# A retention kernel: the low halves of the masked scores are summed on GpSimd before the row-sum matmul

## The chip, the cores and the metric

The kernel runs on one core of one Trainium2 chip, as one program. The metric is the device time of one execution in microseconds. Engines are named PE or TensorE (matrix products), PEld (its weight loads), DVE or VectorE, ACT or ScalarE, POOL or GpSimd, and SP or SyncE (it only issues DMAs here).

## The reference

The input is 8 sequences of 512 tokens with 256 features in float32. Four layers of retention with a feed-forward part run over it, then one mixture of 8 experts. The part that the change touches is in `_retention`:

```python
k, q, v = jnp.split(x @ wkqv, 3, axis=-1)
qkt = jnp.einsum('bid,bjd->bij', q, k) / jnp.sqrt(jnp.float32(d))
row_norm = 1.0 + jnp.sqrt(jnp.arange(s, dtype=x.dtype))[None, :, None]
r = jnp.tril(qkt) / row_norm
denom = jnp.clip(jnp.abs(r.sum(-1, keepdims=True)), 1.0, None)
r = r / denom
return jnp.einsum('bij,bjd->bid', r, v)
```

Each row of the causal scores is divided by the size of its sum. In a layer, the result goes through a gated projection, a group norm over the whole sequence, a residual sum, a GELU feed-forward part and a layer norm:

```python
a, gate = jnp.split(r @ w1 + b1, 2, axis=-1)
y = _groupnorm1(a * jax.nn.silu(gate) @ w2 + b2, gg, gb) + h
f = jax.nn.gelu(y @ wf1 + bf1_) @ wf2 + bf2_
return _layernorm(f + y, lg, lb)
```

## The kernel before

**Precision.** Every float32 operand of a large product is split in two: a high half (ScalarE copies it to the type fp32r) and a low half (the operand less the high half, by VectorE or GpSimd). `mm3` makes a product of three matmuls: high by high, weights high by low, weights low by high.

**Tiling.** A sequence of 512 tokens is one *slot* of a step; a step handles two, slot A (number 0) and slot B (number 1). Four pairs of sequences and four layers make 16 steps. Slot A of a step is interleaved with the later parts of slot B of the step before, and slot B with the later parts of slot A of the same step. Each engine has its own instruction stream, with the order written out in its `body(now, before, seam)`; engines wait for one another on counting semaphores. `first` is step 0 without a step before it, `seam` marks the first step of layers 1 to 3, where new weights are made, and `tail` finishes what the last step left.

**Scores.** `scores` makes the transposed scores in four blocks of 128 keys (partitions) by queries (free axis). Because of the causal mask, block b needs queries from `LO[b]` on only: `LO = [0, 128, 256, 256]`, so widths 512, 384, 256, 256. ScalarE writes the high half `pf_sp[s][0]` (L470), VectorE the low half `pf_sp[s][1]` (L623), and GpSimd's `mask_scores` (L336) clears the part above the diagonal in both halves, block by block, and counts `p_masked[s]` up by one for each block.

**`retain` on TensorE.** It does `weighted_h(0)`, `weighted_h(1)`, then the row sums of the scores with a matrix of ones (`ones_r`, L947: eight matmuls into bank 0, high and low half of each block, `rowsum_psum` when done), then `weighted_h(2)` and `weighted_h(3)`. The row sums wait for `p_masked` of the third block first, later of the fourth. VectorE's `divisor` (L659, L660) takes the row sums, `low_r` the product, `invert` the reciprocal.

**What stands around it.** On TensorE, `retain(A)` is followed by the up projection of B of the step before (it needs `ry_lo` of B, L623 on VectorE), and `retain(B)` by the down projection of A, which takes one chunk of the hidden layer after another as GpSimd's `split_f(A)` (L320, four times) delivers it. Later TensorE does `out_projection(B)`, which needs `tu_lo` of B from VectorE's `gated_products` (`gated` is L677, `low_u` L623).

**GpSimd's order** in a step: `split_h(A)` (L320), mask 0 of A, `rstd_group(B)` (L343), masks 1 to 3 of A, `split_f(B)`, `layernorm_rstd(A)` (L348, L350), `split_h(B)`, `rstd_group(A)`, masks 0 to 3 of B, `split_f(A)`, `layernorm_rstd(B)`, `layernorm_out(A)`, `layernorm_out(B)` (L209, L212 each). `split_weight` makes the low halves of the weights at the seams and in step 0: there the one of `qk` comes first in the step, ahead of `split_h(A)`.

**VectorE** runs `groupnorm_out(B)` (L730 to L740) with `low_y(B)` behind the low halves of A's scores, then `divisor(A)`.

## Time and profile before

| | |
|---|---|
| runs of the kernel before | 2754.56, 2757.17, 2759.98 us (median 2757.17) |
| the profiled execution, first to last instruction | 2757.3 us |
| retention layers, by the order of time | about 0 to 1180 us |
| TensorE busy, whole span | 95% |
| VectorE, ScalarE, GpSimd busy, whole span | 49%, 49%, 47% |

The page of the profile gives busy times, a picture of the span in 40 slices and the costliest groups. Other views of the same trace are used below: stretches (busy time of each engine in a stretch, with the granted clock of TensorE as a share of full speed), waits (who waited for whom, in total, how often, the longest), groups by shape, and the order of time (start, duration, engine, line, operation, result<-operands, shapes, count, and in brackets the idle time before it and what ended it). Durations of GpSimd operations that follow one another overlap by about 0.04 us. Matmuls are pipelined: the time that one costs is from its start to the start of the next.

### The profile page before, as it was taken

Reading aid. Unit: us, or ns where it says so; the run is one execution under the profiler, and the core shown is the slowest. Engines: PE = TensorE matmul, PEld = TensorE weight load, DVE = VectorE, ACT = ScalarE, POOL = GpSimd, SP = SyncE. Lnnn points to the kernel's source line nnn. Section 1 sums busy time; section 2 is a strip of 40 time slices with the busy share of each in tenths; the row PEclk is TensorE's granted clock in tenths of the full one; section 3 lists DMA queues with packets and bytes.
Section 4 is the critical chain, followed back from the end, with each engine's and each line's share of the span. In section 5 each row is a group of like instructions: output and inputs, shape, how many; then the busy total and the mean of one; then the engine's idle time right before and its main releaser. Section 6 shows DMA issues by size and latency. Waiting matters only on the chain.

```text
span 2757.3 us, 42999 instructions
## 1 busy us (share of the span) xinstructions
PE 2625.7 (95%) x14962; PEld 2292.4 (83%) x14962; DVE 1348.6 (49%) x2432; ACT 1361.9 (49%) x2246; POOL 1301.5 (47%) x1142
## 2 busy tenths in 40 slices
PE   7999999999999999949899999999999999999998
PEld 5788778877888788738798998989989989899997
DVE  2677887777777877757812112121121121211233
ACT  3555555566556555525344444444444444444443
POOL 2244554455445544435345445454454454544454
PEclk8999999999999999966999999999999999999999
DMA  4110020002000100042001001000010000000000
GB/s 153 58 31 30 31 69 31 30 31 69 31 30 31 38 31 23 15 133 70 31 0 33 0 0 33 0 29 5 0 34 0 0 33 0 2 0 0 8 23 31
DMA packets 70774, 82.77 MB, mean 30 GB/s; under 512 B 3104, under 2 KB 65696, under 8 KB 70688
## 3 DMA queue, kind: packets, MB, share of 16 engines
q1 hardware_dynamic: 70560, 81.58, 9.0%
q8 instruction: 55, 0.90, 0.1%
q14 instruction: 31, 0.25, 0.0%
q10 hardware_dynamic: 128, 0.03, 0.0%
HBM read 58.27 MB, written 23.33 MB: 30 GB/s over the span
## 4 chain that ended last, share of the span: by engine, by line
issue 24%; POOL 17%; PE 13%; POOLq 1%; DVE 0%; DMA 0%; ACT 0%; ACTq 0%; DVEq 0%; SPq 0%
POOL hid_lo L1257 17%; PE m_ps L1500 4%; PE m_ps L1501 4%; PE m_ps L1502 4%; DMA xh<-h_store 0%; POOLq L1256 0%; PE m_ps L1519 0%; PE m_ps L1526 0%; DVE x L1358 0%; POOLq L1260 0%; ACT x1T_hi L1302 0%; ACT x1Tf L1301 0%; DVE xh L1370 0%; DVE m_stat L1347 0%; POOL rstd L1236 0%
## 5 line engine op out<-in xcount | busy, mean ns | idle before, releaser
L1257 POOL TENSOR_TENSOR hid_lo<-act,hid_hi 128x512 fp32r<-128x512 f32 x512 | 701.5, 1372 | 759.6 <-ACT act L1329 759.5
L1327 ACT ACTIVATE hid_hi<-m_ps,b_e 128x512 fp32r<-128x512 f32 x512 | 353.4, 690 | 811.4 <-PE m_ps L1502 811.2
L1444 DVE TENSOR_TENSOR tile_out<-m_ps,b_bc 128x512 f32<-128x512 f32 x128 | 82.4, 686 | 1015.9 <-PE m_ps L1502 1015.6
L1329 ACT ACTIVATE act<-m_ps,b_e 128x512 f32<-128x512 f32 x512 | 349.7, 683 | 0.0
L1500 PE MATMUL m_ps<-w_even,hid_hi 128*128 128x256 f32 x1024 | 289.6, 283 | 13.5 <-DVE tile_out L1444 13.0
L1502 PE MATMUL m_ps<-w_even,hid_lo 128*128 128x256 f32 x1024 | 290.3, 284 | 0.0
L1501 PE MATMUL m_ps<-w_even,hid_hi 128*128 128x256 f32 x1024 | 290.3, 283 | 0.0
L1500 PE MATMUL m_ps<-w_odd,hid_hi 128*128 128x256 f32 x1024 | 289.1, 282 | 0.8 <-POOL hid_lo L1257 0.6
L1502 PE MATMUL m_ps<-w_odd,hid_lo 128*128 128x256 f32 x1024 | 289.7, 283 | 0.0
L1501 PE MATMUL m_ps<-w_odd,hid_hi 128*128 128x256 f32 x1024 | 289.6, 283 | 0.0
L320 POOL TENSOR_TENSOR pf_lo<-tmp,pf_hi 128x512 fp32r<-128x512 f32 x128 | 161.8, 1298 | 159.4 <-ACT pf_hi L497 159.4
L864 PE MATMUL ps<-ry_hi,w_hi 128*128 128x512 f32 x512 | 207.8, 406 | 14.6 <-DVE ry_lo L623 13.8
L1500 PEld LDWEIGHTS m_ps<-w_even,hid_hi 128*128 128x128 f32 x1024 | 196.1, 192 | 26.6 <-DVE tile_out L1444 13.4
L1500 PEld LDWEIGHTS m_ps<-w_odd,hid_hi 128*128 128x128 f32 x1024 | 195.4, 191 | 14.2 <-POOL hid_lo L1257 3.3
L1500 PE MATMUL m_ps<-x1T_hi,w_even 128*128 (+1 forms) x512 | 203.9, 398 | 1.9 <-issue 1.1
L1501 PEld LDWEIGHTS m_ps<-w_even,hid_hi 128*128 128x128 f32 x1024 | 196.2, 192 | 9.8
L865 PE MATMUL ps<-ry_lo,w_hi 128*128 128x512 f32 x512 | 204.1, 399 | 0.0
L866 PE MATMUL ps<-ry_hi,w_lo 128*128 128x512 f32 x512 | 204.0, 399 | 0.0
L1501 PEld LDWEIGHTS m_ps<-w_odd,hid_hi 128*128 128x128 f32 x1024 | 195.5, 191 | 9.7
L1501 PE MATMUL m_ps<-x1T_lo,w_even 128*128 (+1 forms) x512 | 203.5, 397 | 0.0
L1500 PE MATMUL m_ps<-x1T_hi,w_odd 128*128 (+1 forms) x512 | 202.5, 396 | 0.0
L1501 PE MATMUL m_ps<-x1T_lo,w_odd 128*128 (+1 forms) x512 | 202.3, 395 | 0.0
(176 smaller groups left out, 6305.4 us busy)
## 6 DMA issues: line engine op xcount, KB each, us to landing
h_store<-h_out SPq DMA_DIRECT2D x32, 512.0 KB, 3.2
raw<-in_L_ffn_W SPq DMA_DIRECT2D x16, 1024.0 KB, 6.8
h_in<-h_store SPq DMA_DIRECT2D x24, 512.0 KB, 4.3
h_in<-in_L_attn_x SPq DMA_DIRECT2D x8, 512.0 KB, 5.0
raw<-in_L_attn_Wf SPq DMA_DIRECT2D x8, 512.0 KB, 7.6
acc<-in_L_attn_x SPq DMA_DIRECT2D x8, 512.0 KB, 4.2
xh<-h_store SPq DMA_DIRECT2D x8, 512.0 KB, 5.0
out<-acc SPq DMA_DIRECT2D x8, 512.0 KB, 2.8
```

The costliest lines, as they stand in the source:

```text
L320: nc.gpsimd.tensor_tensor(out=lo, in0=full, in1=f32(hi), op=ALU.subtract).then_inc(done, n)
L864: nc.tensor.matmul(out, w[0], x[0], start=first, stop=False, skip_group_check=True)
L865: nc.tensor.matmul(out, w[0], x[1], start=False, stop=False, skip_group_check=True)
L866: return nc.tensor.matmul(out, w[1], x[0], start=False, stop=last, skip_group_check=True)
L1257: nc.gpsimd.tensor_tensor(out=hid[1][:, j % RING, :], in0=act32[:, j % FULL, :], in1=f32(hid[0][:, j % RING, :]), op=ALU.subtract).then_in ...
L1327: nc.scalar.activation(hid[0][:, j % RING, :], hid_bank(j), ACT.Relu, bias=bias)
L1329: nc.scalar.activation(act32[:, j % FULL, :], hid_bank(j), ACT.Relu, bias=bias).then_inc(hid_relu, 1)
L1444: nc.vector.tensor_tensor(out=tile_out[:, 2 * half:2 * half + 2, :], in0=out_half(parity_t, half).rearrange("p (k d) -> p k d", d=D), in1= ...
L1500: nc.tensor.matmul(out, w[0], x[0], start=first, stop=False, skip_group_check=True)
L1501: nc.tensor.matmul(out, w[0], x[1], start=False, stop=False, skip_group_check=True)
L1502: return nc.tensor.matmul(out, w[1], x[0], start=False, stop=last, skip_group_check=True)
```

## The change

GpSimd adds the low halves of the four masked blocks to one tile `lo_sum` of 512 queries. Behind mask 1, `sum_first_parts` waits for its own masks and for the row sums of the step before, copies the first 128 queries of block 0 (by adding `zeros`) and adds block 0 and block 1 for the other 384. Behind mask 3, `sum_last_parts` adds blocks 2 and 3 in `tail_sum` (256 queries), waits, and adds that to `lo_sum`. On TensorE the four matmuls with low halves go, and one matmul of 512 columns with `lo_sum` is done behind `weighted_h(2)`; `rowsum_psum` is raised by this one. Two new tiles a slot, one of zeros and two semaphores a slot come with it. The ten semaphores of the weights' halves, one for each weight, become two counters.

```diff
+        zeros = sb("zeros", [P, P])
+        lo_sum = slot_tiles("lo_sum", [P, S], F32R)
+        tail_sum = slot_tiles("tail_sum", [P, S // 2])
-        w_hi, w_lo = ({m: sem(f"{m}_{n}") for m in SPANS} for n in ("hi", "lo"))
+        w_hi, w_lo = sem("w_hi"), sem("w_lo")
+
+        def split_count(name, layer):
+            return layer * len(SPANS) + list(SPANS).index(name) + 1
+
+        lo_parts, lo_summed = sems("lo_parts"), sems("lo_summed")
+            nc.gpsimd.memset(zeros[:, :], 0.0).then_inc(pool_consts, 1)
             def split_weight(name, l):
-                pool.wait_ge(w_hi[name], l + 1)
-                low_half(w_full[1][:, SPANS[name]], raw[:, SPANS[name]], w_full[0][:, SPANS[name]], w_lo[name], 1)
+                pool.wait_ge(w_hi, split_count(name, l))
+                low_half(w_full[1][:, SPANS[name]], raw[:, SPANS[name]], w_full[0][:, SPANS[name]], w_lo, 1)
...
                     ins.then_inc(p_masked[s], 1)
+                    if b == 1:
+                        sum_first_parts(s, at)
+                    if b == 3:
+                        sum_last_parts(s, at)
+
+            def low_part(s, b, q):
+                return f32(pf_sp[s][1][:, b, q])
+
+            def sum_first_parts(s, at):
+
+                early, late = slice(0, P), slice(P, S)
+                pool.wait_ge(p_masked[s], at.base + 2)
+                if not isinstance(at.it, int) or at.it:
+                    pool.wait_ge(rowsum_psum[s], at.base)
+                nc.gpsimd.tensor_tensor(out=lo_sum[s][:, early], in0=low_part(s, 0, early), in1=zeros[:, early], op=ALU.add)
+                nc.gpsimd.tensor_tensor(out=lo_sum[s][:, late], in0=low_part(s, 0, late), in1=low_part(s, 1, late),
+                                        op=ALU.add).then_inc(lo_parts[s], 1)
+
+            def sum_last_parts(s, at):
+
+                late = slice(2 * P, S)
+                pool.wait_ge(p_masked[s], at.base + 4)
+                nc.gpsimd.tensor_tensor(out=tail_sum[s][:, :], in0=low_part(s, 2, late), in1=low_part(s, 3, late),
+                                        op=ALU.add).then_inc(lo_parts[s], 1)
+                pool.wait_ge(lo_parts[s], at.it * 2 + 2)
+                nc.gpsimd.tensor_tensor(out=lo_sum[s][:, late], in0=f32(lo_sum[s][:, late]), in1=tail_sum[s][:, :],
+                                        op=ALU.add).then_inc(lo_summed[s], 1)
...
                     pe.wait_ge(p_masked[s], at.base + max(b, 2) + 1)
-                    for half in range(2):
-                        ins = nc.tensor.matmul(bank(s, 0)[:, q], ones_r[:, :], pf_sp[s][half][:, b, q],
-                                               start=b == 0 and half == 0, stop=b == TB - 1 and half == 1,
-                                               skip_group_check=True)
-                ins.then_inc(rowsum_psum[s], U)
+                    nc.tensor.matmul(bank(s, 0)[:, q], ones_r[:, :], pf_sp[s][0][:, b, q],
+                                     start=b == 0, stop=False, skip_group_check=True)
                 weighted_h(2)
+                pe.wait_ge(lo_summed[s], at.it + 1)
+                nc.tensor.matmul(bank(s, 0), ones_r[:, :], lo_sum[s][:, :], start=False, stop=True,
+                                 skip_group_check=True).then_inc(rowsum_psum[s], U)
                 weighted_h(3)
```

The waits of the other engines for weights take the same form as the one shown.

## Rows read from the trace of the kernel before

**Rows 1.** The page: its first line, and TensorE's busy time and share.
```profile
span 2757.3 us, 42999 instructions
...
PE 2625.7 (95%) x14962; PEld 2292.4 (83%) x14962; DVE 1348.6 (49%) x2432; ACT 1361.9 (49%) x2246; POOL 1301.5 (47%) x1142
```

**Rows 2.** Stretches: PE, PEld, DVE, ACT, POOL busy (instructions); PEclk; DMA; GB/s.
```profile
200.00:300.00 100.00, 98.42 (x491) 82.24 (x490) 80.33 (x159) 61.49 (x106) 44.33 (x52) 1.00 0.06 21
```

**Rows 3.** Waits of TensorE, 100 to 1180 us: total, times, longest.
```profile
PE ps L864 <- DVE tu_lo L623: 20.2, 17, 1.9
```

**Rows 4.** TensorE in time, slot B's row sums: start, duration.
```profile
233.68 0.40 PE L947 MATMUL ps<-pf_hi,ones_r 128*128 128x512 f32 x1
...
234.98 0.29 PE L864 MATMUL ps<-pf_hi,h_hi 128*128 128x256 f32 x1
```

**Rows 5.** Groups of GpSimd by shape, 0 to 1200 us: busy, mean ns, idle before.
```profile
L320 POOL TENSOR_TENSOR pf_lo<-tmp,pf_hi 128x512 fp32r<-128x512 f32 x128 | 161.8, 1298 | 159.4 <-ACT pf_hi L497 159.4
...
L212 POOL TENSOR_TENSOR h_out<-z,lnv 128x1024 f32<-128x1024 f32 x30 | 72.1, 2403 | 5.4 <-POOL z L209 3.4
```

**Rows 6.** GpSimd in time, masks 1 (low), 2 (low), 3 (low), slot A.
```profile
261.12 0.29 POOL L336 TENSOR_SCALAR_AFFINE_SELECT pf_lo<-pf_lo 128x128 fp32r<-128x128 f32 x1
...
261.61 0.29 POOL L336 TENSOR_SCALAR_AFFINE_SELECT pf_lo<-pf_lo 128x128 fp32r<-128x128 f32 x1
...
262.21 0.41 POOL L336 TENSOR_SCALAR_AFFINE_SELECT pf_lo<-pf_lo 128x256 fp32r<-128x256 f32 x1
```

**Rows 7.** TensorE in time, `retain` of slot A and the group behind it.
```profile
261.47 0.50 PE L864 MATMUL ps<-pf_hi,h_hi 128*128 128x512 f32 x1 [0.26 <-POOL pf_lo L336]
261.81 0.40 PE L865 MATMUL ps<-pf_lo,h_hi 128*128 128x512 f32 x1
...
263.32 0.39 PE L947 MATMUL ps<-pf_hi,ones_r 128*128 128x512 f32 x1
...
264.60 0.28 PE L864 MATMUL ps<-pf_hi,h_hi 128*128 128x256 f32 x1
...
266.04 0.39 PE L864 MATMUL ps<-ry_hi,w_hi 128*128 128x512 f32 x1
```

**Rows 8.** GpSimd in time, from slot B's mask 1 to the next step.
```profile
229.13 0.30 POOL L336 TENSOR_SCALAR_AFFINE_SELECT pf_lo<-pf_lo 128x128 fp32r<-128x128 f32 x1
...
231.35 5.07 POOL L320 TENSOR_TENSOR pf_lo<-tmp,pf_hi 128x512 fp32r<-128x512 f32 x4 [0.72 <-ACT pf_hi L497]
...
245.23 2.41 POOL L212 TENSOR_TENSOR h_out<-z,lnv 128x1024 f32<-128x1024 f32 x1
247.59 2.86 POOL L320 TENSOR_TENSOR h_lo<-h_in,h_hi 128x1024 fp32r<-128x1024 f32 x1
...
300.27 5.06 POOL L320 TENSOR_TENSOR pf_lo<-tmp,pf_hi 128x512 fp32r<-128x512 f32 x4 [0.71 <-ACT pf_hi L497]
```

**Rows 9.** TensorE in time: the fourth hidden chunk; the out projection.
```profile
238.50 0.39 PE L864 MATMUL ps<-pf_hi,w_hi 128*128 128x512 f32 x1
...
254.02 0.50 PE L864 MATMUL ps<-tu_hi,w_hi 128*128 128x512 f32 x1 [1.03 <-DVE tu_lo L623]
```

**Rows 10.** VectorE in time: operations with two operands in SBUF.
```profile
246.69 1.50 DVE L677 SCALAR_TENSOR_TENSOR tmp<-tmp,lc 128x512 f32<-128x512 f32 x1
...
249.01 1.99 DVE L623 TENSOR_TENSOR tu_lo<-tmp,tu_hi 128x512 fp32r<-128x512 f32 x1 [0.23 <-ACT tu_hi L485]
...
251.70 0.75 DVE L677 SCALAR_TENSOR_TENSOR tmp<-tmp,lc 128x512 f32<-128x512 f32 x1
...
262.73 0.75 DVE L740 SCALAR_TENSOR_TENSOR y<-tmp,gsm,hT_lo 128x512 f32<-128x512 f32 x1
...
264.31 0.69 DVE L623 TENSOR_TENSOR ry_lo<-y,ry_hi 128x512 fp32r<-128x512 f32 x1 [0.17 <-ACT ry_hi L489]
```

**Rows 11.** A long TensorE wait, and the granted clock (0.83) of its stretch.
```profile
651.49 0.77 PE L864 MATMUL ps<-ry_hi,w_hi 128*128 128x512 f32 x1 [2.48 <-DVE ry_lo L623]
...
650.00:660.00 10.00, 8.51 (x30) 0.83 0.00 1
```

More of the change, by code:

```diff
@@ L237, in next_weights @@
             def next_weights(l):
-                for name in SPANS:
-                    sp.wait_ge(w_lo[name], l)
+                sp.wait_ge(w_lo, l * len(SPANS))
                 sp.dma_start(raw[:, 0:FOLD], folded[l]).then_inc(raw_loaded, DMA)
@@ L309, in _ @@
                 pool.sem_inc(h_new[s], U)
+            nc.gpsimd.memset(zeros[:, :], 0.0).then_inc(pool_consts, 1)
             nc.gpsimd.memset(ident[:, :], 0.0).then_inc(pool_consts, 1)
[L311 removed]
+            pool.wait_ge(pool_consts, 2)
             nc.gpsimd.affine_select(out=ident[:, :], in_=ident[:, :], compare_op=ALU.not_equal, fill=1.0,
@@ L316, in _ @@
             nc.gpsimd.memset(mean_w[:, :], 1.0 / (P * DC)).then_inc(pool_consts, 1)
-            pool.wait_ge(pool_consts, 4)
+            pool.wait_ge(pool_consts, 5)
             def low_half(lo, full, hi, done, n):
@@ L412, in _ @@
                 row += n
-            act.wait_ge(pool_consts, 4)
+            act.wait_ge(pool_consts, 5)
             def order_constants():
@@ L431, in empty_fold @@
                 if l == 1:
-                    act.wait_ge(w_lo["qk"], 1)
-                    act.wait_ge(w_lo["vm"], 1)
+                    act.wait_ge(w_lo, split_count("vm", 0))
                 elif l > 1:
@@ L440, in high_weight @@
             def high_weight(name, l):
-                nc.scalar.activation(w_full[0][:, SPANS[name]], raw[:, SPANS[name]], ACT.Copy).then_inc(w_hi[name], 1)
+                nc.scalar.activation(w_full[0][:, SPANS[name]], raw[:, SPANS[name]], ACT.Copy).then_inc(w_hi, 1)
             def next_high_weight(name, l, used, at):
@@ L876, in _ @@
             pe.wait_ge(ident_ready, 1)
-            pe.wait_ge(pool_consts, 4)
+            pe.wait_ge(pool_consts, 5)
             def fold(l):
@@ L911, in project_t @@
                 w = weight("qk", DC)
-                pe.wait_ge(w_lo["qk"], at.layer + 1)
+                pe.wait_ge(w_lo, split_count("qk", at.layer))
                 for k in range(DC):
@@ L955, in gated_projection @@
                 w = weight("vm", DC)
-                pe.wait_ge(w_lo["vm"], at.layer + 1)
+                pe.wait_ge(w_lo, split_count("vm", at.layer))
                 for r, n in ((GATE[0], DC), (VALUE[0], 0), (GATE[1], DC + 1), (VALUE[1], 1)):
@@ L966, in out_projection @@
                 w = weight("m2", DC)
-                pe.wait_ge(w_lo["m2"], at.layer + 1)
+                pe.wait_ge(w_lo, split_count("m2", at.layer))
                 for c in range(DC):
@@ L980, in up_projection @@
                 w = weight("f1", DC)
-                pe.wait_ge(w_lo["f1"], at.layer + 1)
+                pe.wait_ge(w_lo, split_count("f1", at.layer))
                 for k in range(DC):
@@ L990, in down_projection @@
                 w = weight("f2", FC)
-                pe.wait_ge(w_lo["f2"], at.layer + 1)
+                pe.wait_ge(w_lo, split_count("f2", at.layer))
                 for k in hidden:
```

1 line of the change is left out of this document (removed).

## The prediction

> **What bounds the kernel now.** I read the page first. One execution spans 2757.3 us and TensorE is busy for 95% of it [rows 1]; the runs' median is 2757.17 us, so the sum below is made against 2757.3 and needs no correction. The change touches only the retention layers (about the first 1180 us), so I read the stretches next: in a steady 100 us TensorE has work for 98.4 us at full granted clock, GpSimd for 44.3 us [rows 2]. TensorE sets the pace there. Its waits in the steady part come from one place above all, the `tu_lo` that VectorE makes for the out projection of slot B (20.2 us in 17 waits) [rows 3]. Then I read one whole step in order of time (68.9 us, from one `split_f(A)` at 231.35 to the next at 300.27 [rows 8]), engine by engine, around the two calls of `retain`. The reader should see two things. In slot A TensorE already waits for the mask, by 0.26 us [rows 7]. In slot B GpSimd goes from the mask straight to `split_f`, a chain of back-to-back work that ends only 20 us later with `h_lo` [rows 8]. So GpSimd's 44% does not tell that it has room: its free time lies elsewhere.
>
> **Removed.** Each `retain` has eight row-sum matmuls, starting at 233.68 and followed by the next group at 234.98: 1.30 us [rows 4]. High and low halves have the same widths, so the four low ones (512 + 384 + 256 + 256 = 1408 columns) take 0.65 us, 0.46 ns a column. One of 512 columns comes back, 0.24 us. Net 0.41 us per call, 32 calls (16 steps, two slots): 13 us, 0.5%. All of it lies on the bounding engine, so this is the most that can be won.
>
> **Added on GpSimd.** A tensor_tensor takes 2403 ns on 1024 columns and 1298 on 512 [rows 5]; the line through both is 0.2 us + 2.15 ns a column. That gives 0.47 us (128 columns), 1.02 (384) and 0.75 (256, twice). Before the first sum and between dependent ones GpSimd waits for its own last write; the same wait of L212 for L209 cost 3.4 us in its fifteen slot A instances, 0.23 each [rows 5], and I take 0.2. So `sum_first_parts` costs 0.2 + 0.47 + 1.02, less an overlap of 0.04: 1.65 us, ahead of masks 2 and 3. `sum_last_parts` costs 0.2 + 0.75 + 0.2 + 0.75 = 1.9 us. Both: 3.55 us. The wait for the last step's row sums is over a whole step earlier and costs nothing. Everything behind them in GpSimd's queue moves by that, unless it waited for another engine anyway.
>
> **Slot A, no other effect counted.** Mask 1 ends at 261.41, mask 2 at 261.91, mask 3 at 262.62 [rows 6]. Masks 2 and 3 move by 1.65 to 263.56 and 264.27; the sum is ready at 264.27 + 1.9 = 266.17. TensorE wants mask 2 at 263.32 [rows 7], so starts 0.3 late at 263.62; it refills (after a wait the second matmul starts 0.34 behind the first, at 261.81 [rows 7], where 0.24 is usual: 0.1 lost), meets mask 3 at 264.33, and is through `weighted_h(2)` (half of the 1.44 us between 264.60 and 266.04, 0.72 us [rows 7]) at about 265.3. It then stands until 266.23 for `lo_summed`, and ends `weighted_h(3)` at 266.23 + 0.34 + 0.72 = 267.29 against 266.04 before: +1.25 us, saving included. Behind it stands all of TensorE's queue, first the up projection of B.
>
> **Slot A with VectorE in the way.** The rows show the two engines blocking one another where VectorE reads two operands in SBUF: L677 took 1.50 us at 246.69, where L212 ran until 247.64, and 0.75 at 251.70 without GpSimd beside it; `tu_lo` at 249.01 took 1.99 where its like at 264.31 took 0.69, and ended just after `h_lo`; and that `h_lo`, of 1024 columns as L212 is, took 2.86 instead of 2.40 [rows 5, 8, 10]. The new sums fall between 261.6 and 266.2, just where VectorE runs `groupnorm_out(B)` and `low_y(B)`: `y<-tmp,gsm,hT_lo` at 262.73 and `ry_lo<-y,ry_hi` at 264.31, each with two operands in SBUF [rows 10], and each twice. If only the tensor_tensors contend, one 0.65 us block hits the last sum: about +1.7. If masks contend too, `y` slips in before mask 2's second half (mask 2 at 264.4, mask 3 at 265.1), `ry_lo` before the tail sum, the second `y` before the last: `lo_summed` near 267.8, retain ends near 268.9, +2.9. I take the middle, +2.3 us; ends 1.25 and 2.9. VectorE's own delay (up to 1.5 us) is covered: the divisor and the up projection wait for TensorE's later times.
>
> The Trainium skill, page "SBUF — State Buffer", section "Who interferes with whom", says that a DVE instruction with two SBUF inputs contends with a GpSimd instruction that reads SBUF, and that the later one fully blocks. By that rule, which the rows just named agree with, masks count as well, and slot A would come out at the upper end, 2.9; it speaks against this change.
>
> **Slot B, directly.** Masks 0 and 1 are done at 229.43 and mask 3 at 231.35 - 0.72 = 230.63 [rows 8]; 1.65 later that is 232.3, before the row sums at 233.68 [rows 4]. The sum is ready at 230.63 + 3.55 = 234.2 and wanted at 233.68 + 0.65 + 0.72 = 235.05. Nothing waits, and the 0.41 is won there. But `split_f(A)` starts at 234.1 instead of 231.35, 2.8 later, since only 0.72 us of idle time stood before it [rows 8]. At 1.25 us apart its four chunks end at 235.4, 236.65, 237.9, 239.2. The down projection, now begun at 236.0, takes one each 0.7 us (three matmuls of 0.24), and would want the fourth at 238.50 - 0.41 = 238.1 [rows 9]; it gets it at 239.2 and is 0.7 to 0.85 us later than before. I take 0.85.
>
> **Slot B, what comes after.** GpSimd's whole chain is 2.8 us late. `h_lo` began at 247.59 and ended at 250.45 [rows 8]; now it ends near 253.7 (2.8 and half a microsecond of blocks by VectorE). `gated(1)`, L677 at 251.70, ran just behind it and unhindered [rows 10]; now it is asked for near 252.1, amid `h_lo`, and runs at 253.6 to 254.35. From its end to TensorE's going on with `tu_lo` were 1.57 us (252.45 to 254.02 [rows 9, 10]); so TensorE goes on at 255.9 instead: +1.9 us in all for slot B. This takes in the 0.85, since the wait ends by GpSimd's time whatever TensorE did before. Without the blocks it is 0.85.
>
> **Elsewhere.** In step 0 slot A is followed by folds that wait for a DMA: nothing. Slot B of step 0: 0.85. At the three layer seams `w_lo` of `qk` is at the end of the late chain and holds `project_t` by some 2 us, of which the later `tu_lo` wait absorbs all but 0.3: 1 us in all. The joined counters `w_hi`/`w_lo` count in the order in which the weights are made anyway, and one more memset of 0.2 us lies under the first loads: nothing. The tail has no `retain`, and the expert mixture merely starts later.
>
> **Sum.** 15 steps x (2.3 + 1.9) + 0.85 + 1 = 65 us; the time is 2757.3 + 65 = 2822 us, +2.4%. A measurement of this kernel can tell about 0.2% (5.5 us) from no change.
>
> **Rivals.** (1) Queue order alone, no blocking between the engines: 15 x (1.25 + 0.85) + 0.85 + 1 = 33 us, 2790 us. For it: nothing in the trace overlaps the very pair. Against it: the three lengthened rows. (2) On top of the forecast the granted clock falls. In the trace a TensorE wait of 2.48 us is followed by a window of 10 us with 0.83 granted [rows 11]; 0.17 of 10 us at half clock means 3.4 us at the lower level and 1.7 us lost. The wait for `tu_lo` grows from 1.0 to over 2 us, so one such fall a step is possible: 15 x 1.7 = 25 more, 2847 us. Against it: waits up to 1.9 us leave 1.00 now [rows 2, 3]. (3) Faster: the sums finish before they are wanted, and TensorE keeps its 13 us: 2744 us. The place is the last wait of `retain(A)` and the fourth chunk of `split_f(A)`; it decides when all four sums take under about 2.1 us instead of 3.55. Operations of the same kind and type say no. (4) The two halves cancel: A loses 0.4 and B keeps 0.4, within 5 us of 2757; it needs sums of some 2.4 us. That the low matmuls do not go away is no case: the code leaves no choice.
>
> **How the numbers follow.** Forecast 0.53, rival 1 0.20, rival 2 0.15, rival 3 0.06, rival 4 0.06. The forecast's own span, from slot A's ends and 1.5 to 2.1 for slot B, is 2798 to 2834. The range reaches to rivals 1 and 2 with some room: 2784 to 2852. Slower by over 0.2%: 0.88; within: 0.06; faster: 0.06.
>
> **What would show it.** Right: in slot A a TensorE wait of 1 to 2.5 us for `lo_summed` ahead of the last ones-matmul, one of some 0.3 to 1 us for mask 2 ahead of the row sums; in slot B waits for `split_f`'s `pf_lo` in the down projection; the `tu_lo` wait at 2 us and more, with L677 lengthened by `h_lo`; a step of 73 us for 68.9. Wrong: `pf_lo` and `lo_sum` sums much shorter than 0.75 us; GpSimd starting `split_f(A)` less than 2 us late; L740 and `ry_lo` in slot A at their old 0.75 and 0.69 with undelayed masks (then rival 1); granted clock below 1.00 in steady stretches (then rival 2).

## The result, and the profile after

| | before | after |
|---|---|---|
| median | 2755.95 us | 2821.15 us |
| range of the runs | 2754.56 to 2759.98 (4) | 2813.55 to 2824.7 (4) |
| span of the profiled execution | 2757.3 us | 2811.8 us |

The ratio is 1.0232, with a 95% interval from 1.0219 to 1.0244. The changed kernel is 2.3% slower; the forecast was 2822 us. The median was met, but not every term of the sum was. The profiled execution is the fastest of the four, so two differences are kept apart below: 54.5 us between the two traces, and 65.2 us between the medians. One of the six executions of y5_busy_wait took 9070.51 us, for a reason that is not known, and is left out of everything below.

The page of the kernel after, its first line and the engines' totals (to be held against [rows 1]):

```profile
span 2811.8 us, 43058 instructions
...
PE 2640.5 (94%) x14866; PEld 2286.6 (81%) x14866; DVE 1377.8 (49%) x2432; ACT 1361.4 (48%) x2246; POOL 1413.0 (50%) x1271
```

TensorE has 96 matmuls fewer, three for each of 32 calls. GpSimd has 111.5 us more to do, on 50% of the span instead of 47%: the engine with time to spare took the work, and the kernel lost. So the waits come next, TensorE's from 100 to 1240 us (total, times, longest; [rows 3] is the same view before):

```profile
PE ps L898 <- DVE tu_lo L657: 25.0, 16, 1.9
PE ps L984 <- POOL lo_sum L373: 17.7, 15, 1.4
...
PE ps L898 <- POOL w_lo L328: 8.3, 3, 2.8
PE ps L980 <- POOL pf_lo L344: 6.7, 15, 0.5
```

The second and the fourth are new: once in each step TensorE waits for the masks behind the first sums, and for the last sum. The first stood at 20.2 us before, and `w_lo` at the seams at 1.3.

**Slot A.** TensorE after, in time (start, duration, and in brackets the wait before it), to be held against [rows 7]:

```profile
263.91 0.50 PE L898 MATMUL ps<-pf_hi,h_hi 128*128 128x512 f32 x1 [0.24 <-POOL pf_lo L344]
...
266.45 1.09 PE L980 MATMUL ps<-pf_hi,ones_r 128*128 128x512 f32 x4 [0.52 <-POOL pf_lo L344]
...
269.63 0.47 PE L984 MATMUL ps<-lo_sum,ones_r 128*128 128x512 f32 x1 [1.38 <-POOL lo_sum L373]
...
270.65 0.39 PE L898 MATMUL ps<-ry_hi,w_hi 128*128 128x512 f32 x1
```

From 263.91 to the up projection at 270.65 are 6.74 us; before, 261.47 to 266.04, 4.57. So slot A costs 2.17 us. GpSimd and VectorE in the same microseconds:

```profile
263.94 0.46 POOL L362 TENSOR_TENSOR lo_sum<-pf_lo,zeros 128x128 fp32r<-128x128 f32 x1
264.36 1.02 POOL L363 TENSOR_TENSOR lo_sum<-pf_lo 128x384 fp32r<-128x384 f32 x1
...
265.58 0.82 POOL L344 TENSOR_SCALAR_AFFINE_SELECT pf_lo<-pf_lo 128x128 fp32r<-128x128 f32 x1
...
267.18 1.18 POOL L370 TENSOR_TENSOR tail_sum<-pf_lo 128x256 f32<-128x256 f32 x1
268.44 1.05 POOL L373 TENSOR_TENSOR lo_sum<-lo_sum,tail_sum 128x256 fp32r<-128x256 f32 x1
```

```profile
265.50 0.75 DVE L774 SCALAR_TENSOR_TENSOR y<-tmp,gsm,hT_lo 128x512 f32<-128x512 f32 x1
...
267.08 0.69 DVE L657 TENSOR_TENSOR ry_lo<-y,ry_hi 128x512 fp32r<-128x512 f32 x1 [0.17 <-ACT ry_hi L523]
267.69 1.22 DVE L774 SCALAR_TENSOR_TENSOR y<-tmp,gsm,hT_lo 128x512 f32<-128x512 f32 x1
```

The mask at 265.58 takes 0.82 us where its like took 0.29 [rows 6], beside VectorE's `y` at 265.50. `tail_sum` takes 1.18 beside `ry_lo`, and the last sum 1.05 beside the second `y`, which itself takes 1.22 instead of 0.75.

**Slot B.** GpSimd after, from mask 1 of slot B on (against [rows 8]):

```profile
230.40 0.29 POOL L344 TENSOR_SCALAR_AFFINE_SELECT pf_lo<-pf_lo 128x128 fp32r<-128x128 f32 x1
230.78 0.46 POOL L362 TENSOR_TENSOR lo_sum<-pf_lo,zeros 128x128 fp32r<-128x128 f32 x1
...
233.49 0.74 POOL L370 TENSOR_TENSOR tail_sum<-pf_lo 128x256 f32<-128x256 f32 x1
234.31 0.74 POOL L373 TENSOR_TENSOR lo_sum<-lo_sum,tail_sum 128x256 fp32r<-128x256 f32 x1
235.01 5.04 POOL L328 TENSOR_TENSOR pf_lo<-tmp,pf_hi 128x512 fp32r<-128x512 f32 x4
...
251.52 2.83 POOL L328 TENSOR_TENSOR h_lo<-h_in,h_hi 128x1024 fp32r<-128x1024 f32 x1
...
307.26 5.03 POOL L328 TENSOR_TENSOR pf_lo<-tmp,pf_hi 128x512 fp32r<-128x512 f32 x4
```

Here nothing contends: the two 256-column sums take 0.74 each, and from the end of mask 1 (230.69) to the end of the last sum (235.05) are 4.36 us, where slot A has 5.64 (263.85 to 269.49). The difference, 1.28, is the three lengthened operations of slot A (0.53 + 0.44 + 0.31). One step is 307.26 - 235.01 = 72.25 us, for 68.92 between the same two rows of [rows 8]: 3.33 us more. The end of the chain, TensorE and VectorE after (against [rows 4], [rows 9] and [rows 10]):

```profile
234.95 0.81 PE L980 MATMUL ps<-pf_hi,ones_r 128*128 128x512 f32 x4
...
240.10 0.50 PE L898 MATMUL ps<-pf_hi,w_hi 128*128 128x512 f32 x1 [0.27 <-POOL pf_lo L328]
...
256.48 0.51 PE L898 MATMUL ps<-tu_hi,w_hi 128*128 128x512 f32 x1 [1.81 <-DVE tu_lo L657]
```

```profile
252.80 2.10 DVE L711 SCALAR_TENSOR_TENSOR tmp<-tmp,lc 128x512 f32<-128x512 f32 x1
255.73 0.69 DVE L657 TENSOR_TENSOR tu_lo<-tmp,tu_hi 128x512 fp32r<-128x512 f32 x1 [0.82 <-ACT tu_hi L519]
```

`gated(1)` is asked for amid `h_lo` and takes 2.10 us instead of 0.75. From the row sums to the out projection TensorE now needs 256.48 - 234.95 = 21.53 us, before 254.02 - 233.68 = 20.34: slot B costs 1.19.

**Where the 54.5 us lie.** Three of the 15 steps between the first and the last `split_f(A)` are seams. They grew by 3.0, 2.0 and 1.9 us. The other twelve grew by 50.8 in all: 40.0 is twelve times the 3.33 of an undisturbed step, and 10.8 is on top. In the first step `split_f(A)` comes 1.8 earlier, and what follows the last step takes 1.5 less; both were left unexplained. The 10.8 goes with the granted clock. One stretch with a low clock, and the matmul after a wait in it:

```profile
553.60 0.50 PE L898 MATMUL ps<-tu_hi,w_hi 128*128 128x512 f32 x1 [1.85 <-DVE tu_lo L657]
...
550.00:560.00 10.00, 8.15 (x35) 0.83 0.29 98
```

The 0.17 that is missing here to full clock is 1.7 us of 10. The same 1.7 us is missing every time, in one stretch of 10 us or shared between two neighbours. Each such time is called a *fall* below. The falls from 90 to 1150 us are counted by dividing all that is missing there by 1.7. Before there were 2 falls, both at seams; now there are 10, and two more up to the last `split_f(A)` at 1204.99. Of these 12, four lie in the seams and eight in seven of the other twelve steps. Those seven are 12.1 us longer than 3.33 us a step explains, 1.0 to 2.6 each; the three other steps from the third on are within 0.1 us of it, and the first two are 0.8 and 0.5 shorter.

### The profile page after: what moved, and what is told of

Its sections match the earlier page's. It is cut to its first block, busy times and chain, and to the rows that moved or that the text cites. A ratio compares the mean times of both kernels' runs of the same rounds, so it can differ in the third digit from the quotient of the medians.

```text
span 2811.8 us, 43058 instructions
## 1 busy us (share of the span) xinstructions
PE 2640.5 (94%) x14866; PEld 2286.6 (81%) x14866; DVE 1377.8 (49%) x2432; ACT 1361.4 (48%) x2246; POOL 1413.0 (50%) x1271
## 4 chain that ended last, share of the span: by engine, by line
issue 24%; POOL 17%; PE 13%; POOLq 1%; DVE 1%; DMA 0%; ACT 0%; ACTq 0%; DVEq 0%; SPq 0%
POOL hid_lo L1291 17%; PE m_ps L1534 4%; PE m_ps L1535 4%; PE m_ps L1536 4%; DMA xh<-h_store 0%; POOLq L1290 0%; PE m_ps L1553 0%; DVE x L1392 0%; PE m_ps L1560 0%; POOLq L1294 0%; ACT x1T_hi L1336 0%; ACT x1Tf L1335 0%; DVE xh L1404 0%; DVE m_stat L1381 0%; POOL rstd L1270 0%
```

## The experiments

Times are medians; ratios are to the kernel before on the same chip. "Step" is one without a fall and away from the seams; "falls" are counted as above.

| kernel | us | ratio (95%) | step | falls |
|---|---|---|---|---|
| before | 2754 to 2756 | | 68.92 | 2 |
| after | 2821.15 | 1.0232 (1.0219 to 1.0244) | 72.25 | 10 |
| x4_slot_a_only | 2789.14 | 1.0127 (1.0111 to 1.0142) | 71.07 | 2 |
| z1_slot_b_only | 2785.38 | 1.0110 (1.0095 to 1.0125) | 70.13 | 13 |
| x2_sums_unread | 2794.4 | 1.0142 (1.0127 to 1.0158) | 70.93 | 12 |
| x3_fills | 2812.36 | 1.0208 (1.0192 to 1.0224) | 72.3 | 8 |
| y1_sums_last | 2817.07 | 1.0232 (1.0215 to 1.0248) | 71.9 | 12 |
| y5_busy_wait | 2813.3 | 1.0212 (1.0199 to 1.0225) | 71.8 to 72.4 | 6 |
| x1_high_only | 2746.18 | 0.9963 (0.9949 to 0.9976) | 68.27 | 4 |
| y2_two_blocks | 2755.04 | 0.9993 (0.9984 to 1.0001) | 68.93 | 2 |
| y3_late_row_sums | 2754.28 | 0.9993 (0.9984 to 1.0002) | 68.85 | 2 |
| z2_quarters | 2804.63 | 1.0176 (1.0160 to 1.0191) | 71.4 | 12 |
| z5_before_ln_quarters | 2747.18 | 0.9972 (0.9961 to 0.9983) | 68.15 | 5 |
| z4_combined | 2740.2 | 0.9943 (0.9930 to 0.9957) | 67.73 | 4 |

The diffs are against the changed kernel, the one of z5_before_ln_quarters against the kernel before.

### Each slot alone

x4_slot_a_only sums in slot A only; slot B has its eight matmuls back.

```diff
-                    if b == 1:
+                    if s == A_ and b == 1:
                         sum_first_parts(s, at)
-                    if b == 3:
+                    if s == A_ and b == 3:
                         sum_last_parts(s, at)
...
+                    if s == A_:
+                        nc.tensor.matmul(bank(s, 0)[:, q], ones_r[:, :], pf_sp[s][0][:, b, q],
+                                         start=b == 0, stop=False, skip_group_check=True)
+                    else:
+                        for half in range(2):
+                            ins = nc.tensor.matmul(bank(s, 0)[:, q], ones_r[:, :], pf_sp[s][half][:, b, q],
...
                 weighted_h(2)
+                if s == A_:
+                    pe.wait_ge(lo_summed[s], at.it + 1)
```

> The change in slot A only; slot B keeps its eight row-sum matmuls and GpSimd makes no sums for it. Theory: slot A alone loses 2.2 us a step (15 steps): 2786 to 2792 us, and the rest of the 65 us is slot B's. Rival: slot B's late chain carries the loss, and slot A alone is within 10 us of before (up to 2766).

Measured: +2.15 us a step and 34 us in all, within what was expected. TensorE's waits from 100 to 1180 us:

```profile
PE ps L993 <- POOL lo_sum L373: 19.9, 15, 1.4
PE ps L898 <- DVE tu_lo L657: 16.9, 15, 1.6
```

The wait for `lo_sum` is that of the full change, and the one for `tu_lo` is no longer than before. There are 2 falls, as before, though not the same ones: before they follow waits of 2.48 us for `ry_lo` at two seams, here two of the 15 waits for `lo_sum`. So slot A's 2.17 us stand by themselves, and they bring few falls.

z1_slot_b_only is the mirror image.

```diff
-                    if b == 1:
+                    if s == B_ and b == 1:
                         sum_first_parts(s, at)
-                    if b == 3:
+                    if s == B_ and b == 3:
                         sum_last_parts(s, at)
...
+                    if s == B_:
+                        nc.tensor.matmul(bank(s, 0)[:, q], ones_r[:, :], pf_sp[s][0][:, b, q],
...
```

> The change in slot B only; slot A as before, without sums. Theory: the two slots add up. The undisturbed step of the changed kernel is 3.33 us longer than before, slot A alone makes it 2.15 longer, so slot B alone makes it 1.18 longer, 70.1 us, and the time is 15 x 1.2 and some 5 us for seams and clock more: 2774 to 2784 us. Rival: the slots share a wait (one loss hides the other), and slot B alone costs over 2 us a step: 2790 or more.

Measured: an undisturbed step is +1.21, so the two slots add up (2.15 + 1.21 = 3.36 for 3.33). The total came out just above the expected range, because not all steps are undisturbed: six take 71.7 us, 1.57 more, and two, each the first behind a seam, 72.9; each of the eight has one fall. One such place, stretches of TensorE (length, busy and instructions, granted clock, DMA share, GB/s) and in time:

```profile
465.00:470.00 5.00, 5.00 (x27) 1.00 0.56 195
470.00:475.00 5.00, 3.18 (x9) 0.75 0.34 105
475.00:480.00 5.00, 5.00 (x30) 0.91 0.00 0
480.00:485.00 5.00, 4.72 (x29) 1.00 0.00 0
```

```profile
471.93 0.50 PE L898 MATMUL ps<-tu_hi,w_hi 128*128 128x512 f32 x1 [1.82 <-DVE tu_lo L657]
```

TensorE was fully busy until it waited 1.82 us for `tu_lo`; in the stretch of that wait and the one behind it part of the time was granted at 1.2 GHz instead of 2.4, and then it was 1.00 again. Of the 13 falls eight follow a wait for `tu_lo`, and five follow waits at the seams, for `w_lo` (2.8 us each, where the three took 1.3 together before) and for `ry_lo` (2.48). So most of the falls of the change come with slot B.

### Queue, blocking, or the wait on TensorE

x2_sums_unread keeps all sums on GpSimd, but TensorE does its eight matmuls as before and doesn't wait for `lo_sum`.

```diff
-                    nc.tensor.matmul(bank(s, 0)[:, q], ones_r[:, :], pf_sp[s][0][:, b, q],
-                                     start=b == 0, stop=False, skip_group_check=True)
+                    for half in range(2):
+                        ins = nc.tensor.matmul(bank(s, 0)[:, q], ones_r[:, :], pf_sp[s][half][:, b, q],
...
                 weighted_h(2)
-                pe.wait_ge(lo_summed[s], at.it + 1)
-                nc.tensor.matmul(bank(s, 0), ones_r[:, :], lo_sum[s][:, :], start=False, stop=True,
```

> The changed kernel with all four sums on GpSimd, but TensorE does the eight row-sum matmuls of before and never waits for lo_sum (the sums are not used). Theory: masks 2 and 3 of slot A stay late (some 0.6 us a step) and the late chain of slot B stays (1.2 us a step); what goes is the wait for lo_sum (1.4 us a step) and the saving. 15 x 1.8 and some us at the seams: 2785 to 2795 us. Rival: all of the loss is TensorE's wait for lo_sum, and the time is that of before, 2756, within 5 us.

Measured: +2.0 us a step, 40 us in all, as expected. The sums cost that much by being made on GpSimd, read or not; the remaining 1.3 us a step is what waiting for `lo_sum` costs more than the saved matmuls give.

x3_fills puts memsets where the sums were. They read nothing, and the row sums leave the low halves out.

```diff
+            def fill(s, at, part, *tiles, again):
+                for n, group in enumerate((tiles, again)):
+                    if n:
+                        pool.wait_ge(pad_done[s], at.it * 3 + part + 1)
...
+                            ins = nc.gpsimd.memset(tile[:, c:c + P], 0.0)
...
-                nc.gpsimd.tensor_tensor(out=lo_sum[s][:, early], in0=low_part(s, 0, early), in1=zeros[:, early], op=ALU.add)
-                nc.gpsimd.tensor_tensor(out=lo_sum[s][:, late], in0=low_part(s, 0, late), in1=low_part(s, 1, late),
...
+                fill(s, at, 0, f32(lo_sum[s][:, :]), tail_sum[s], zeros, again=(tail_sum[s],)).then_inc(lo_parts[s], 1)
```

> In place of the four sums GpSimd makes fills of about the same total length (memsets, which read nothing from SBUF), with the same waits ahead and behind; the low halves are left out of the row sums. Theory of blocking: with fills VectorE's operations with two SBUF operands and GpSimd don't block each other in slot A, so masks and lo_sum come 1.3 us a step earlier than in the changed kernel: about 20 us less than its 2821, near 2801. Rival (queue order alone): the same time as the changed kernel, 2821, within 5 us.

Measured: 9 us less than the changed kernel by the medians and 7 by the ratios, whose intervals just overlap, where about 20 was expected. The trace shows why. GpSimd from the end of mask 1 to the last fill, first slot B, then slot A (the last mask row ahead of the fills, ending at 232.36 and 266.13, and the last fill):

```profile
232.07 0.29 POOL L344 TENSOR_SCALAR_AFFINE_SELECT pf_lo<-pf_lo 128x128 fp32r<-128x128 f32 x1
...
237.13 0.20 POOL L360 MEMSET zeros<- 128x128 f32 x1 [0.15 <-POOL zeros L360]
...
265.84 0.29 POOL L344 TENSOR_SCALAR_AFFINE_SELECT pf_lo<-pf_lo 128x128 fp32r<-128x128 f32 x1
...
270.96 0.20 POOL L360 MEMSET zeros<- 128x128 f32 x1 [0.15 <-POOL zeros L360]
```

The fills were meant to be as long as the sums, but in slot B they take 4.97 us for 4.36. In slot A they take 5.03: only 0.06 more than in slot B, where the sums took 1.28 more. So fills are hardly hindered by the same VectorE work. The step as a whole is no shorter (72.3 us for 72.25), since slot B pays 0.63 us for the longer fills (22.16 us from the row sums to the out projection, for 21.53); what is left of the gain in the total goes with fewer falls (8 for 10). So blocking is read from slot A's `retain` and not from the total. With 0.6 us more in the queue, `retain` of slot A still takes 0.6 less than with the sums:

```profile
266.19 0.50 PE L906 MATMUL ps<-pf_hi,h_hi 128*128 128x512 f32 x1 [0.24 <-POOL pf_lo L344]
...
271.31 0.47 PE L992 MATMUL ps<-lo_sum,ones_r 128*128 128x512 f32 x1 [1.01 <-POOL zeros L360]
...
272.33 0.39 PE L906 MATMUL ps<-ry_hi,w_hi 128*128 128x512 f32 x1
```

That is 6.14 us, 1.57 above before. Less the 0.6 that the fills are too long, the order of the queue alone costs slot A about 1.0, and the blocking about 1.2 of the 2.17.

y1_sums_last does all sums behind the last mask.

```diff
-                    if b == 1:
-                        sum_first_parts(s, at)
                     if b == 3:
+                        sum_first_parts(s, at)
                         sum_last_parts(s, at)
```

> The changed kernel with all four sums behind the last mask, so that no mask is late. Theory: the wait for the masks in slot A (0.5 us a step) goes, but lo_sum comes no earlier, so TensorE waits that much longer for it; the length of GpSimd's queue decides, not the place of the sums in it: within 6 us of the changed kernel's 2821, and slot A's retain as long as there (6.7 us from its second group to the up projection). Rival: the late masks are a cost of their own, and 15 x 0.6 us come out: 2812.

Measured: 1.0232, the ratio of the changed kernel, and 2817 us. The wait for the mask goes and the one for `lo_sum` takes its place (17.7 us in the changed kernel):

```profile
PE ps L983 <- POOL lo_sum L372: 32.0, 15, 2.2
```

The step is 0.35 us shorter, and 12 falls for 10 take that back. Where the first sums stand therefore hardly matters; what counts is when the last one is done, and that TensorE wants it at once.

### The clock

y5_busy_wait lets TensorE work through its wait for `tu_lo`: six matmuls whose result is overwritten.

```diff
+                if s == B_:
+                    pe.wait_ge(u_lo[s], at.base + 2)
+                    for again in range(2):
+                        mm3(bank(s, OUT[0]), both(w, ALL, 0, cols(0)), both(tu_sp[s], ALL, 0), True, False)
```

> The changed kernel; ahead of the out projection of slot B TensorE does its first product of three matmuls twice more (six matmuls, 1.4 us, the result is the same), which fall into its 1.8 us wait for tu_lo. Theory: the stretches with a granted clock under 1.00, a dozen in the changed kernel against two before, come of that wait, and with TensorE busy in it they go: undisturbed steps stay at 72.25 us, the time falls by 8 to 13 us to about 2808 to 2813. Rival: the falls of the clock have nothing to do with it; the time stays at 2821 or grows a little (seams with a shorter wait).

Measured: TensorE's waits from 100 to 1180 us have

```profile
PE ps L898 <- DVE tu_lo L657: 4.7, 11, 0.5
```

for the changed kernel's 21.1 in 14 in the same stretch. The falls go from 10 to 6: in the changed kernel four follow a wait for `tu_lo`, here none does, and the six that are left follow waits that this run doesn't fill, three for `lo_sum` (1.39 us) and three at the seams. The mean granted clock of its runs is 0.973 to 0.974 where that of the changed kernel's is 0.965 to 0.969, and the time is 8 us less by the medians and 5.5 by the ratios, with steps of the same length (71.8 to 72.4 us in both, without a fall) but two seams that are 3 us longer. The intervals of the two ratios overlap, so the gain in time is likely but not certain; that of the clock is clear. The wait for `tu_lo` is thus a cause of falls, but not the only one.

### What the saving on TensorE is worth

x1_high_only has neither sums nor low matmuls: the row sums leave the low halves out.

```diff
-                    if b == 1:
-                        sum_first_parts(s, at)
-                    if b == 3:
-                        sum_last_parts(s, at)
...
-                pe.wait_ge(lo_summed[s], at.it + 1)
-                nc.tensor.matmul(bank(s, 0), ones_r[:, :], lo_sum[s][:, :], start=False, stop=True,
-                                 skip_group_check=True).then_inc(rowsum_psum[s], U)
```

> Leaves out the low halves from the row sums altogether: no sums on GpSimd, no low matmuls (the row sums are those of the high halves alone). Theory: TensorE sets the pace, so its 0.65 us a call, 32 calls, come out in full: some 21 us less than before, about 2735 us; the 0.41 us a call that the change itself saves would then be worth 13 us. Rival: the retention step is held by chains of VectorE and GpSimd, and the time stays within 5 us of before, 2751 to 2761.

Measured: 0.65 us a step instead of 1.3, and 9 us in all instead of 21. TensorE in time, slot B's row sums and out projection:

```profile
229.44 0.81 PE L976 MATMUL ps<-pf_hi,ones_r 128*128 128x512 f32 x4
249.77 0.50 PE L894 MATMUL ps<-tu_hi,w_hi 128*128 128x512 f32 x1 [1.68 <-DVE tu_lo L653]
```

VectorE in time, the `gated` ahead of the first `tu_lo`, which now falls amid GpSimd's work:

```profile
241.79 2.14 DVE L707 SCALAR_TENSOR_TENSOR tmp<-tmp,lc 128x512 f32<-128x512 f32 x1
```

That is 20.33 us for 20.34 before: slot B's 0.65 us went into a longer wait for `tu_lo` (1.68 for 1.03), which goes by GpSimd's time. Only slot A's saving becomes time. Of the 13 us of the change about 6 were ever to be had (15 x 0.41).

y2_two_blocks has GpSimd add only blocks 2 and 3 (one operation of 256 columns, behind the last mask).

```diff
-                nc.gpsimd.tensor_tensor(out=tail_sum[s][:, :], in0=low_part(s, 2, late), in1=low_part(s, 3, late),
-                                        op=ALU.add).then_inc(lo_parts[s], 1)
-                pool.wait_ge(lo_parts[s], at.it * 2 + 2)
-                nc.gpsimd.tensor_tensor(out=lo_sum[s][:, late], in0=f32(lo_sum[s][:, late]), in1=tail_sum[s][:, :],
+                nc.gpsimd.tensor_tensor(out=lo_sum[s][:, late], in0=low_part(s, 2, late), in1=low_part(s, 3, late),
...
+                    if b < 2:
+                        nc.tensor.matmul(bank(s, 0)[:, q], ones_r[:, :], pf_sp[s][1][:, b, q],
+                                         start=False, stop=False, skip_group_check=True)
```

> GpSimd sums only blocks 2 and 3 (one tensor_tensor of 256 columns behind the last mask, 0.74 us), TensorE does the low halves of blocks 0 and 1 as before and one matmul of 256 columns in place of two. Theory: the sum ends before TensorE wants it and split_f(A) is some 0.1 us late only; slot A wins 0.12 us a step, slot B nothing that shows: 2753 against 2755, no change that can be told. Rival: even one sum beside VectorE's operations with two SBUF operands delays the group norm's chain: 5 us or more slower than before.

Measured: no change, as expected, 68.93 us a step. The joined counters are in this kernel too, so they cost nothing either. About 0.8 us in GpSimd's queue is covered in both slots (slot B had 0.72 idle ahead of `split_f` [rows 8]); 3.1 is not.

y3_late_row_sums sums in slot A alone, last of all, and does the matmul with `lo_sum` six matmuls into the up projection.

```diff
-                    if b == 1:
+                    if s == A_ and b == 3:
                         sum_first_parts(s, at)
-                    if b == 3:
                         sum_last_parts(s, at)
...
                 weighted_h(2)
+                weighted_h(3)
+
+            def low_row_sums(s, at):
                 pe.wait_ge(lo_summed[s], at.it + 1)
...
+                        if meanwhile and k == 0 and n == 1:
+                            meanwhile()
...
-                    up_projection(B_, before)
+                    up_projection(B_, before, lambda: low_row_sums(A_, now))
```

> Slot A only: all sums behind the last mask, and TensorE takes lo_sum not within retain but six matmuls into the up projection of B, some 2 us later; slot B as before. Theory: TensorE's wait for lo_sum (1.4 us a step) was all that slot A lost apart from the masks, so with the sum wanted after it is there slot A keeps its 0.41 us a step: 6 us faster than before, 2749. Rival: VectorE's group norm and the divisor, delayed by the sums, come onto the path (the gate's product waits for the reciprocal): same as before or up to 10 us slower.

Measured: 0.11 us a step instead of 0.41; in all 2 us instead of 6, which is below what the total can show. The sums' whole price in slot A is gone, but the last sum ends only at 265.47, and the late matmul starts at 265.62 where TensorE was free at 265.39. With the slower start behind a wait some 0.3 of the 0.41 is lost.

### A way out

z2_quarters is the changed kernel with `h_lo` in four operations of 256 columns.

```diff
-                low_half(h_sp[s][1][:, :, :], h_in[s][:, :, :], h_sp[s][0][:, :, :], h_lo[s], U)
+                for k in range(TB):
+                    ins = nc.gpsimd.tensor_tensor(out=h_sp[s][1][:, k, :], in0=h_in[s][:, k, :], in1=f32(h_sp[s][0][:, k, :]),
+                                                  op=ALU.subtract)
+                ins.then_inc(h_lo[s], U)
```

> The changed kernel, but h_lo is made by four GpSimd operations of 256 columns instead of one of 1024. Theory: slot B loses because VectorE's operations with two SBUF operands stand behind a 2.4 us GpSimd operation on the path to tu_lo; with quarters they wait for 0.7 us at most, tu_lo comes about 1 us a step earlier: 15 us less than the changed kernel, 2803 to 2810. Rival: TensorE waits for the end of GpSimd's late chain itself and not for the single operation; four operations take 0.5 us longer than one, so 2821 or up to 2828.

Measured: about 0.8 us a step less than the changed kernel. `gated(1)`, VectorE in time:

```profile
252.64 1.15 DVE L714 SCALAR_TENSOR_TENSOR tmp<-tmp,lc 128x512 f32<-128x512 f32 x1
```

It waits for one quarter, not for the rest of 1024 columns (2.10), and from the row sums to the out projection TensorE needs 20.88 us instead of 21.53. This is the direct proof that `gated(1)` was blocked by `h_lo`. The falls are not fewer (12): nine of them follow waits at or just behind the seams, where quarters make `w_lo` no earlier, and three follow waits for `lo_sum`. None follows a wait for `tu_lo` in a plain step, where those are now 1.1 to 1.5 us.

z5_before_ln_quarters is the kernel before with quarters in `h_lo` and in both operations of `layernorm_out`; it has nothing of the change.

```diff
-            ops.tensor_tensor(out=z[s][:, :, :], in0=z[s][:, :, :], in1=gain, op=ALU.mult).then_inc(z_gained[s], U)
+            for k in range(TB):
+                ins = ops.tensor_tensor(out=z[s][:, k, :], in0=z[s][:, k, :], in1=gain[:, k, :], op=ALU.mult)
+            ins.then_inc(z_gained[s], U)
...
-                low_half(h_sp[s][1][:, :, :], h_in[s][:, :, :], h_sp[s][0][:, :, :], h_lo[s], U)
+                for k in range(TB):
+                    ins = nc.gpsimd.tensor_tensor(out=h_sp[s][1][:, k, :], in0=h_in[s][:, k, :], in1=f32(h_sp[s][0][:, k, :]),
...
```

> The kernel before, with h_lo and both GpSimd layer norm outputs in quarters of 256 columns, nothing else. Theory: in the kernel before L677 loses 0.75 and tu_lo 1.3 us to one GpSimd operation each, on the path to TensorE's 1.0 us wait for tu_lo; with quarters most of that wait goes, about 1 us a step: 2740 us. Rival: the longer chain of GpSimd meets two more operations of VectorE and takes back what it gave: 2750 to 2760.

Measured: 0.8 us a step and 7 us in all, half of what was expected. VectorE in time, against the 1.50 and 1.99 of [rows 10]:

```profile
240.40 0.99 DVE L684 SCALAR_TENSOR_TENSOR tmp<-tmp,lc 128x512 f32<-128x512 f32 x1
...
242.22 1.02 DVE L630 TENSOR_TENSOR tu_lo<-tmp,tu_hi 128x512 fp32r<-128x512 f32 x1 [0.23 <-ACT tu_hi L492]
```

GpSimd beside it, and behind that TensorE's wait for `w_lo`, 100 to 1180 us:

```profile
237.19 2.83 POOL L210 TENSOR_TENSOR z<-z,lnv 128x256 f32<-128x256 f32 x4
...
240.10 3.74 POOL L215 TENSOR_TENSOR h_out<-z,lnv 128x256 f32<-128x256 f32 x4
```

```profile
PE ps L871 <- POOL w_lo L324: 8.5, 3, 2.9
```

Four quarters take GpSimd 2.83 us alone where one operation took 2.40 [rows 5], and 3.74 with VectorE in between. At the seams the weights' low halves come at the end of that chain: 8.5 us of waits for 1.3. Two of the seams are 2.4 and 1.2 us longer than before for it, and there are 5 falls for 2. This ate part of the gain.

z4_combined joins y3_late_row_sums (now nine matmuls into the up projection) with the quarters of z5_before_ln_quarters.

```diff
+                        if meanwhile and k == 0 and n == 2:
+                            meanwhile()
```

> Slot A only, with all sums behind the last mask and lo_sum taken nine matmuls into the up projection of B (no wait left there), and h_lo and both GpSimd layer norm outputs in quarters of 256 columns. Theory: 0.4 us a step from slot A's row sums and 1 us a step from the shorter blocks, 21 us: 2735. Rival: GpSimd, whose chain gets about 2 us longer by the quarters, holds VectorE just as often: the time is 2750 to 2756.

Measured: 2740.2 us, 0.57% less than before, the best of all, though 14 us for the 21 that were expected. Its step is 0.4 us shorter than that of z5_before_ln_quarters, which is the saving of 0.41 in one slot; the quarters do the rest.

## Why the prediction was right, point by point

**What bounds the kernel.** Right: the chain of GpSimd behind the masks of slot B, and slot A's wait for the masks. Neither can be read from the busy shares.

**Removed.** The 0.41 us a call is right for TensorE's work, and "the most that can be won" was wrong. In slot B TensorE's time is set by `tu_lo` further on; x1_high_only shows 0.65 us of matmuls leaving there with 0.01 us to show for it. The forecast itself rested on it in slot A only, since its slot B counted to the end of that wait. Rival 3 rested on it in both slots; its 13 us should have been some 6.

**Added on GpSimd.** The line of 0.2 us + 2.15 ns a column gave 0.47, 1.02 and 0.75; measured 0.46, 1.02 and 0.74. The wait for its own last write was mis-sized: 0.2 was taken, 0.08 to 0.09 measured (230.69 to 230.78, 233.41 to 233.49, 234.23 to 234.31). The 0.23 that it was taken from is one of two values for the same pair of operations: in slot B of the kernel before it is 0.13 (L209 ends at 245.10, L212 starts at 245.23). All sums of slot B cost 3.12 us (1.48 + 1.64) instead of 3.55, and `split_f(A)` came 2.39 late instead of 2.8 (counted from the row sums).

**Slot A.** Predicted 2.3, measured 2.17 (2.15 alone). TensorE waits 0.52 for mask 2 (0.3 predicted) and 1.38 for `lo_sum`. The order of the queue makes up about 1.0 of it (1.25 predicted) and the blocking 1.2 (1.05 predicted); x3_fills tells them apart. Masks do contend, as one of the two ends assumed.

The Trainium skill, page "SBUF — State Buffer", section "Who interferes with whom", was right on the mechanism: it has a DVE instruction with two SBUF inputs contend with a GpSimd instruction that reads SBUF, not with one that only writes it. The mask at 0.82 for 0.29, `tail_sum` at 1.18 for 0.74 and L711 at 2.10 for 0.75 agree with it, and so does the absence of blocking with fills, which read nothing. Its reading as "the upper end, 2.9" was too high by 0.7 here: the three blocks fell where that end put them (on mask 2, the tail sum and the last sum), but the two on the sums lasted 0.44 and 0.31 instead of some 0.65, and the sums themselves were shorter.

**Slot B.** This step failed in size: predicted 1.9, measured 1.19. The mechanism is as told, `gated(1)` amid `h_lo`, and from its end to TensorE's going on are 1.58 us (1.57 predicted). But `h_lo` ends 2.63 us later than before (19.40 us behind the row sums, for 16.77), not 3.25: 0.41 of this is the sums' smaller price, and 0.2 that VectorE held up the chain for 0.24 us and not for half a microsecond. The direct part, the fourth chunk, was 0.33 (240.10 - 234.95 = 5.15, for 4.82) and not 0.85, for the same reason; it was absorbed as the text said.

**Elsewhere.** The three seams were to grow by 4.5 each and grew by 2.3 on average, and that with 4 falls in them instead of 2. The wait for `w_lo` of 2 us is there (8.3 in three, for 1.3), but more of the other losses hide behind it than was thought. The joined counters cost nothing that the steps show.

**The sum, and what made up for it.** Per undisturbed step 3.33 us for 4.2. With this alone and the seams as they are, the profiled execution would be some 44 us longer (40.0 + 6.9, less the 3.3 of the first step and of what follows the last), about 2801. Rival 2 is what filled the gap, in part. It was given 0.15, with waits "up to 1.9 us leave 1.00 now" as the reason against. That reading was wrong. Up to 1165 us the longest wait for `tu_lo` before is 1.64 us, and most are 1.0; the only one of 1.9 comes at the end of the retention layers, and the clock falls right at its end (0.62 granted from 1170 to 1171 us, and 0.68 in the stretch shown, which holds the next fall too):

```profile
1170.41 0.79 PE L864 MATMUL ps<-tu_hi,w_hi 128*128 128x512 f32 x1 [1.94 <-DVE tu_lo L623]
...
1170.00:1180.00 10.00, 4.18 (x11) 0.68 0.00 0
```

With slot B's sums in the kernel there are 10 to 13 falls (8 with fills in their place, 6 with the wait filled), without them 2 (x4_slot_a_only, y2_two_blocks, y3_late_row_sums) to 5. A fall in a plain step costs 1.57 us (z1_slot_b_only; 1.7 predicted), and there was not one a step but eight in twelve, 12.1 us of which the two shorter first steps leave 10.8. The rest, from 54.5 to 65.2 us, is between executions: an execution's time is 1.7 us above its span, so the trace of before stands for 2759.0 us, 3.1 above the median (the text took span and median for the same, which was off by that much), and the one of after for 2813.55, 7.6 below its median. The other three executions of after have a lower mean clock (0.965 to 0.967 for 0.969), which fits more falls, but no trace of them shows it. The total was thus met by luck, through errors of opposite sign: the steps were put 10 us (12 x 0.87) and the seams 7 us too high, and the clock (10.8 us) and the 10.7 us between the profiled executions and the medians were left out. The mechanisms of both slots held, and the loss was foreseen for the right reasons; that the forecast came within 1 us of it was chance. (The lower end of the forecast's own span is 2800 by its terms, 15 x 2.75 + 1.85 = 43, and not 2798; nothing hangs on it.)

**Rivals.** Rival 1 is out: L344, L370 and L373 are lengthened, and with fills in their place the lengthening is gone. Rivals 3 and 4 are out: sums of 3.1 us are above the 2.1 and 2.4 from which they decide; y2_two_blocks, with 0.8 us, is the point at which losses and gains do cancel.

**Left open.** Why a wait of 1.8 us is followed by a fall in some steps and not in others that look alike was not settled. In x1_high_only none of the eight waits for `tu_lo` of 1.67 to 1.73 us is followed by one, and two of the three of 1.82 and more are. The waits for `lo_sum`, shorter than that, are followed by a fall now and then (2 of 15 in x4_slot_a_only). Nor is it known why `split_f(A)` of the first step comes 1.8 us earlier.

## What to carry to other kernels

An engine busy for half of the time may have no room at the place where the work is put: follow its queue from the new instruction to the next one that somebody waits for, and count only the idle time in between (0.72 us here, for 3.1 of work). A saving on the bounding engine becomes time only if the next wait behind it doesn't end by another engine's clock; leave the work out altogether to see what there is to win, before paying for it. Where VectorE operations with two operands in SBUF wait behind long GpSimd ones, shorter GpSimd operations can be worth more than the change that was planned (0.8 us a step here, for 0.4).

## What the runs showed of the hardware that was not expected

- GpSimd's mask operation contends with VectorE as its sums do, which the prediction had left open: 0.82 us for 0.29 beside an operation with two operands in SBUF. Fills don't: 0.06 us between the two slots, for 1.28.
- A blocked VectorE operation gets in between two GpSimd operations that follow back to back: 1.15 us for 2.10 with quarters (z2_quarters). The quarters cost GpSimd 0.43 us for 1024 columns (2.83 for 2.40).
- GpSimd's wait for its own last write costs 0.08 to 0.09 us behind the masks and sums of 128 to 256 columns, where it had been 0.23 behind one of 1024 in slot A and 0.13 behind its like in slot B. What sets it was not tested.
- Over all fourteen traces, from 90 to 1150 us: of TensorE's waits for `tu_lo`, 58 lasted 1.77 us or more, and 29 of them were followed by a fall of the granted clock; 72 lasted 1.00 to 1.73 us, and none was. It isn't the length alone: of 57 waits for `lo_sum` of 0.93 to 1.39 us, which come some 13 us behind one for `tu_lo`, 10 were followed by a fall. In a plain step a fall cost 1.57 us.
